# Turned keys, one-pass rounding and a new order in the merged attention of a six-sublayer decoder

## What is computed

```python
# causal self-attention in BitNet form, 16 query heads and 4 key heads of 32
def bitlinear(x, W):
    sw = mean(abs(W)) + 1e-05
    Wq = clip(round(W / sw), -1, 1) * sw
    sx = 127.0 / clip(max(abs(x), axis=-1), 1e-05, None)
    return (clip(round(x * sx), -128, 127) / sx) @ Wq.T
q, k, v = bitlinear(x, Wq), bitlinear(x, Wk), bitlinear(x, Wv)   # then rope on q and k
out = bitlinear(softmax(q @ k.T / sqrt(32), causal) @ v, Wo)

# gated attention to the memory of the same sequence (ctx), 16 heads of 32, mask on the memory
xr = rmsnorm(x, norm_w)
q, k, v = xr @ wq.T, ctx @ wk.T, ctx @ wv.T
out = sigmoid(xr @ wg.T) * (softmax(q @ k.T * 32 ** -0.5, mask) @ v @ wo.T)

# experts: 8 groups of 8, top 8 of 64 per token
soft = softmax(where(flat == 0, -1e9, flat))           # routing weights of a group
xg = x + soft @ mask_up_w                              # the "mover", 8 rows a group
y = sum over groups: scalar * ((silu(xg @ gate.T) * (xg @ up.T)) @ down.T)
```

## Time and profile before

| | |
|---|---|
| time, median of 3 runs (lowest to highest) | 3289.37 us (3287.53 to 3293.52) |
| profiled execution, its own time | 3293.45 us |
| its span, mean granted clock of PE | 3291.6 us, 0.939 |
| PE busy | 2859.2 us, 87% |
| PE's weight loads busy | 1596.8 us, 49% |
| DVE busy | 1998.1 us, 61% |
| ACT busy | 1622.2 us, 49% |
| POOL busy | 1209.3 us, 37% |
| 512-column matmul in an expert group, mean of 768 | 379 ns |
| `stage_moe`: first work of DVE | 2343.75 us |
| `stage_moe`: POOL's low part of the first weights ends, scores are ready | 2387.0 us, 2394.8 us |

### The profile page before, as it was taken

One profiled execution on the slowest core, in us unless ns is written; L12 is line 12 of the kernel. 1 busy time (PEld: TensorE's weight loads), 2 busy tenths in 40 slices (PEclk: granted clock), 3 DMA queues, 4 the chain that ended last, 5 costly groups with the idle time before them and its releaser, 6 DMA issues. The chain is left out here.

```text
span 3291.6 us, 48914 instructions
## 1 busy us (share of the span) xinstructions
PE 2859.2 (87%) x16626; PEld 1596.8 (49%) x16626; DVE 1998.1 (61%) x3760; ACT 1622.2 (49%) x3728; POOL 1209.3 (37%) x1236
## 2 busy tenths in 40 slices
PE   6789877999999997899368888877569999999998
PEld 4676744555555553344245444543434444444443
DVE  5778978877887876774678778764532212222224
ACT  7999955555555553642467666654321221212111
POOL 4888967554554541342321111100402221222211
PEclk8999988999999999999579999998779999999999
DMA  4111122000000001200300000000000000000001
GB/s 150 54 42 40 49 77 79 7 4 7 7 4 7 7 0 56 98 1 1 108 12 8 8 7 7 8 11 1 31 30 30 30 30 1 30 30 30 1 1 51
DMA packets 29926, 94.83 MB, mean 29 GB/s; under 512 B 3862, under 2 KB 4246, under 8 KB 26519
## 3 DMA queue, kind: packets, MB, share of 16 engines
q1 hardware_dynamic: 29718, 92.26, 8.2%
HBM read 87.79 MB, written 4.46 MB: 28 GB/s over the span
## 5 line engine op out<-in xcount | busy, mean ns | idle before, releaser
L710 POOL TENSOR_TENSOR m_aTl<-m_prod,m_aTh 128x512 bf16<-128x512 f32 x96 | 110.9, 1156 | 704.6 <-ACT m_aTh L764 704.6
L923 DVE TENSOR_TENSOR m_prod<-m_bank,m_gated 128x512 f32<-128x512 f32 x96 | 66.4, 692 | 497.1 <-ACT m_gated L762 497.1
L1893 POOL TENSOR_TENSOR s_state<-s_state,s_ct 128x512 f32<-128x512 f32 x256 | 326.6, 1301 | 85.0 <-DVE s_state L2068 83.1
L2068 DVE TENSOR_TENSOR_SCAN s_state<-s_decay,s_psd 128x512 f32<-128x512 f32 x256 | 301.9, 1209 | 68.3 <-PE s_psd L2213 35.0
L762 ACT ACTIVATE m_gated<-m_bank 128x512 f32<-128x512 f32 x96 | 57.2, 596 | 575.6 <-PE m_bank L1007 575.6
L1005 PE MATMUL m_bank<-m_xTh,m_wh 128*128 128x512 bf16 x768 | 291.1, 379 | 0.0
L1006 PE MATMUL m_bank<-m_xTl,m_wh 128*128 128x512 bf16 x768 | 291.1, 379 | 0.0
L1007 PE MATMUL m_bank<-m_xTh,m_wl 128*128 128x512 bf16 x768 | 291.1, 379 | 0.0
L2213 PE MATMUL s_psd<-ident,s_v 128*128 128x128 f32 x1024 | 165.3, 286 | 42.8 <-DVE s_state L2068 22.4
L1969 ACT ACTIVATE s_decay<-s_dt,s_nega 128x508 f32<-128x508 f32 x256 | 182.0, 712 | 20.5 <-DVE s_state L2068 20.3
L1982 ACT ACTIVATE s_v<-s_uT,s_bT 128x512 f32<-128x512 f32 x256 | 182.5, 714 | 0.8 <-PE s_psd L2213 0.7
(11 more groups left out here) (502 smaller groups left out, 8058.9 us busy)
## 6 DMA issues: line engine op xcount, KB each, us to landing
m_stage<-in_moe_w_dram SPq DMA_DIRECT2D x8, 2352.0 KB, 8.5
s_ct<-ssm_bc SPq DMA_DIRECT2D x64, 256.0 KB, 3.1
X<-in_x_dram SPq DMA_DIRECT2D x4, 1024.0 KB, 11.2
a_cf<-in_ctxT_dram SPq DMA_DIRECT2D x16, 256.0 KB, 2.6
a_wstage<-in_xa_wq_dram SPq DMA_DIRECT2D x8, 512.0 KB, 3.5
a_wstage<-in_xa_wo_dram SPq DMA_DIRECT2D x8, 512.0 KB, 3.8
f_wstage<-in_ffn_wg_dram SPq DMA_DIRECT2D x4, 1024.0 KB, 7.4
f_wstage<-in_ffn_wu_dram SPq DMA_DIRECT2D x4, 1024.0 KB, 5.7
```

The source lines that it names most:

```text
L1893: pool.tensor_tensor(h, h, ct[t % 4][:, s * P:(s + 1) * P].unsqueeze(1).broadcast_to([P, KB, P]), ALU.mult).then_inc(weighted, 1)
L2068: dve.tensor_tensor_scan(state[i % RING][:, :], decay[t % 2][:, s, :, :].rearrange("p m t -> p (m t)"), ps_d[i % 2][:, :], 0.0, ALU.mult, ...
```

## The change

Three things in `stage_pair`. First, the memory half's keys and queries come out of PE already turned (`turned_product`: 48 matmuls of 128 columns, the weight matrix as the stationary operand); `krow`, `qrow`, `turn_keys` and `turn_queries` are gone. High and low part are one pass of 128 x 512 each, into a dense buffer `kT`, and SP moves four row blocks of it into the block-diagonal buffer by DMA (`place_keys`). The causal half's rotated key is written to `krd`, four blocks of 128 columns with head h at columns 32h of block h and zeros elsewhere; PE turns the four blocks (`turn_key`), and high and low part are one pass of all 128 rows each. Second, `PairQuantizer`: ACT scales and rounds in one pass (`round`), DVE does both clips in one (`clip`), ACT takes `ROUND` off as before. Third, the hand-written orders: `memory_end` goes from quarter 2 to quarter 3, `values` and `key_low` of the causal half, `keys_low`, `queries_low`, `memory_values`, `gate_output`, `norm_apply`, `quantize_x` and the vector parts of both norms change their quarter or their place in it.

In `stage_moe`, `group_rows` is cut into `soft_rows`, done two thirds of a quarter earlier, and `mover_rows`; the mover of group 0 is made during the routing; the last `down_tile`s are spread over blocks 1 and 2 of the last quarter; and the last four tiles are normalised and stored one by one (`tail`) in place of one quarter.

```diff
+        def tiles_behind(q, b, last):
+
+            if last and q == TQ - 1:
+                return ((), (0, 1), (2, 3))[b]
+            return ((0, 1), (2, 3), ())[b]
...
-            for q in range(TQ):
+            for q in range(TQ - 1):
                 sp.wait_ge(ln.normed.sem, ln.normed.at(q))
                 sp.dma_start(out[4 * q:4 * q + 4].rearrange("s p d -> p s d"), fr.X[:, 4 * q:4 * q + 4, :]).then_inc(stored, 16)
-            sp.wait_ge(stored, 16 * TQ)
+            for t in range(4):
+                sp.wait_ge(tail.steps.sem, tail.steps.at(t))
+                sp.dma_start(out[SEQS - 4 + t], fr.X[:, SEQS - 4 + t, :]).then_inc(stored, 16)
+            sp.wait_ge(stored, 16 * (TQ + 3))
...
+                        if q == 2 and b == 0 and not last:
+                            soft_rows(g + 1, 1 - j)
                     if q == 0 and not last:
                         w_high_part(g + 1, 1 - j)
                     if q == 2 and not last:
-                        group_rows(g + 1, 1 - j)
+                        mover_rows(g + 1, 1 - j)
...
+            dve.wait_ge(padded, 4)
...
+            mover_rows(0, 0)
...
+                    if q == 1 and not last:
+                        soft_rows(g + 1, 1 - j)
                     if q == 2 and not last:
-                        group_rows(g + 1, 1 - j)
+                        mover_rows(g + 1, 1 - j)
...
-            ln.vector_end(dve, TQ - 2)
             for t in range(4):
                 add_tile(G - 1, TQ - 1, t, 1)
-            dve.wait_ge(added.sem, added.at(G - 1))
-            ln.vector(dve, TQ - 1)
-            ln.vector_end(dve, TQ - 1)
+                if t == 0:
+                    ln.vector_end(dve, TQ - 2)
+                dve.wait_ge(added.sem, added.at(G - 1, 4 * (TQ - 1) + t + 1))
+                tail.statistics(dve, t)
+                if t:
+                    tail.vector_end(dve, t - 1)
+            tail.vector_end(dve, 3)
...
-        self.kdh = [sb(f"{tag}_kdh{j}", [P, key_groups, 4, P], BF16, st) for j in range(2)]
-        self.kdl = [sb(f"{tag}_kdl{j}", [P, key_groups, 4, P], BF16, st) for j in range(2)]
+        self.kd = [sb(f"{tag}_kd{j}", [P, 2, 4, key_groups, P], BF16, st) for j in range(2)]
...
+                   (self.kd[p][:, 0, :, k, :], self.kd[p][:, 1, :, k, :]), False, True)
...
+            def place_keys(n, j):
+                sp.wait_ge(mk_low.sem, mk_low.at(n))
+                if late(n, 2):
+                    sp.wait_ge(mcore.scored.sem, mcore.scored.at(n - 2))
+                for h in range(4):
+                    rows = slice(32 * h, 32 * h + 32)
+                    sp.dma_start(mcore.kd[j][rows, :, h, :, :], kT[rows, :, :, :]).then_inc(mcore.k_ready.sem, 16)
...
+                    place_keys(2 * i + j, j)
+                    context(2 * i + j + 2)
...
-                for g in range(4):
-                    rows = slice(32 * g, 32 * g + 32)
-                    a = act.activation(core.kdh[j][rows, 0, g, :], bank[2][rows, 0:P], ACT.Copy)
-                a.then_inc(k_high.sem, 1)
+                act.activation(core.kd[j][:, 0, :, 0, :].rearrange("p h t -> p (h t)"), bank[2][:, :], ACT.Copy).then_inc(k_high.sem, 1)
...
-                act.activation(krow[:, :], bank[0][:, :], ACT.Copy).then_inc(k_row.sem, 1)
-
-            def queries(n):
-                act.wait_ge(mproj.sem, mproj.at(n, 3))
-                if late(n, 1):
-                    act.wait_ge(mq_turned.sem, mq_turned.at(n - 1))
-                act.activation(qrow[:, :], bank[2][:, :], ACT.Copy, scale=PairCore.HW ** -0.5).then_inc(q_row.sem, 1)
+                    act.wait_ge(mcore.k_ready.sem, mcore.k_ready.at(n - 1))
+                act.activation(kT[:, 0, :, :].rearrange("p c t -> p (c t)"), bank[0][:, :], ACT.Copy).then_inc(mk_high.sem, 1)
+
+            def queries_high(n, j):
+                act.wait_ge(mproj.sem, mproj.at(n, 2))
+                act.activation(mcore.qTh[j][:, :, :].rearrange("p g t -> p (g t)"), bank[2][:, :], ACT.Copy,
+                               scale=PairCore.HW ** -0.5).then_inc(mq_high.sem, 1)
...
+                            qx.round(act, s + 2, fr.X[:, s + 2, :])
...
+                            queries_high(m + 1, o)
+                    if g == 2:
                         if live(s - 1):
-                            copy_output(s - 1)
+                            qo.scalar(act, s - 1)
                         if live(m + 1):
-                            gates(m + 1, o)
+                            memory_values(m + 1, o)
+                    if g == 3 and live(m + 2):
+                        squares(m + 2)
...
+                    if g == 1 and live(s + 2):
+                        qx.scalar(act, s + 2)
+                    if g == 2 and live(m + 2):
+                        context_high(m + 2, p)
+                    if g == 3 and live(m + 1):
+                        gates(m + 1, o)
...
-                for g in range(4):
-                    rows = slice(32 * g, 32 * g + 32)
-                    a = dve.tensor_tensor(core.kdl[j][rows, 0, g, :], bank[2][rows, 0:P], core.kdh[j][rows, 0, g, :], ALU.subtract)
-                a.then_inc(core.k_ready.sem, 1)
+                dve.tensor_tensor(core.kd[j][:, 1, :, 0, :].rearrange("p h t -> p (h t)"), bank[2][:, :],
+                                  core.kd[j][:, 0, :, 0, :].rearrange("p h t -> p (h t)"), ALU.subtract).then_inc(core.k_ready.sem, 1)
...
+                dve.tensor_tensor(kT[:, 1, :, :].rearrange("p c t -> p (c t)"), bank[0][:, :],
+                                  kT[:, 0, :, :].rearrange("p c t -> p (c t)"), ALU.subtract).then_inc(mk_low.sem, 1)
...
-                    if g == 1 and live(s - 1):
-                        output(s - 1)
+                    if g == 1:
+                        if live(m + 1):
+                            keys_low(m + 1)
+                        if live(s - 1):
+                            output(s - 1)
+                        if live(s + 2):
+                            qx.clip(dve, s + 2)
                     if g == 2:
+                        if live(s - 1):
+                            qo.clip(dve, s - 1)
                         if live(s - 2):
-                            ln.vector_end(dve, s - 2)
+                            ln.statistics(dve, s - 2)
                         if live(s + 1):
                             query_low(s + 1, o)
-                    if g == 3 and live(s + 3):
-                        quantize_x(s + 3, o)
+                            key_low(s + 1, o)
+                    if g == 3 and live(s - 2):
+                        ln.vector_end(dve, s - 2)
                     if live(s):
                         core.low_part(dve, s, g)
                     if g == 0:
                         if live(s + 1):
                             rotate_keys(s + 1, o)
+                            values(s + 1, o)
                         if live(s - 1):
                             core.divide(dve, s - 1, o)
-                        if live(s + 1):
-                            values(s + 1, o)
-                    if g == 1 and live(s - 2):
-                        ln.statistics(dve, s - 2)
-                    if g == 2 and live(s + 1):
-                        key_low(s + 1, o)
+                    if g == 3 and live(s + 3):
+                        quantize_x(s + 3, o)
 
                     if live(m) and (g < 3 or live(m + 1)) or g == 3 and live(m + 1):
                         mcore.maxima(dve, *following(m, g, p)[:2])
                     if g == 0 and live(m - 1):
                         mcore.divide(dve, m - 1, o)
-                    if g == 1 and live(m - 1):
-                        low(oTl[:, :], bank[1][:, :], oTh[:, :], o_high, m - 1, o_low)
-                    if g == 2 and live(m - 1):
-                        gate_output(m - 1, o)
+                    if g == 1:
+                        if live(m - 1):
+                            low(oTl[:, :], bank[1][:, :], oTh[:, :], o_high, m - 1, o_low)
+                        if live(m - 2):
+                            mln.vector_end(dve, m - 2)
                     if g == 3:
-                        if live(m - 1):
-                            mln.vector_end(dve, m - 1)
                         if live(m + 2):
                             norm_mean(m + 2)
+                        if live(m - 1):
+                            gate_output(m - 1, o)
                     if live(m):
                         mcore.low_part(dve, m, g)
                     if g == 0 and live(m + 1):
                         low(nTl[o][:, :], bank[1][:, :], nTh[o][:, :], n_high, m + 1, n_low)
+                    if g == 1 and live(m + 1):
+                        queries_low(m + 1, o)
+                    if g == 2 and live(m + 1):
                         memory_values(m + 1, o)
-                    if g == 1 and live(m + 1):
-                        keys_low(m + 1, o)
-                    if g == 2:
-                        if live(m + 1):
```

(51 more changed lines are left out.)

301 lines of the change are left out of this document (157 added, 144 removed).

## The result

The changed kernel takes 3197.76 us (median of four runs, 3190.47 to 3201.64), the kernel before 3291.30 beside it. The ratio is 0.9714, 95% interval 0.9694 to 0.9735: 93.5 us less. The forecast was 3204, range 3158 to 3238.

A forecast was written before the change was run, and what follows sets the result against it. No engine full: full attention turns bound by queue order and cross-engine waits, late turns by latency, expert groups by PE's waits. Attention -59 and experts -27 make -86 us, from 3293.5 to 3208, as median 3204; range 3158 to 3238.

The forecast's parts named there:

- The keys: Key and query pieces in stage_pair: ACT -3.4 us, DVE -2.6 us a turn; turned matmuls 0.056 us each, DMAs cost nothing.
- Quantisation: Two quantisers in stage_pair: DVE loses a 0.53 us pass in each, -1.0 us; ACT gains two of 0.60.
- The ring: Waits across DVE and PE in a full stage_pair turn: 13.2, 11.1 and 13.4 us, sum 37.7 against 40.7.
- The stretches around it: Other stage_pair turns: two behind the full ones -5 us, two before -4, four early -4, three late -20.7.
- Groups: Seven expert groups in stage_moe: PE's waits of 1.58 and 0.75 us go, -16.3 us in all.
- Start of the experts: Before the first expert group: soft rows' turning earlier, -6.9 us; net with DVE's added wait -5.3 (-3 to -8).
- four memsets: Before the first expert group: DVE waits for all of POOL's memsets, +1.6 us.
- End: Last tiles of stage_moe: last `X` at 3283.1 for 3287.0, last store 2.6 us for 4.3; -5.6 us (-4 to -7).
- B: stage_pair order better than the schedule: DVE keeps only present waits, 34.5 us a turn, total 3156 us; chance 0.22.
- C: PE's 2.4 us idling in quarter 1 slows the Q product: +2 us on thirteen turns, total 3230; chance 0.13.
- D: Turned products in stage_pair limited by weight loads of 0.098 us each: +2.0 us a product, total 3242; chance 0.08.
- E: Key DMAs land late and hold the scores of quarter 3: slower than before, total 3316 us; chance 0.03.

The follow-up runs named there:

- keys_pieces: Changed kernel with the memory half's turned key placed by four 32-row pieces on ACT and on DVE, without kT and DMAs: 3252.61 us, ratio 0.9896.
- wide: Changed kernel with the memory half's K and Q as twelve 512-column matmuls each, keys and queries not turned: 3193.10 us, ratio 0.9702.
- quant_old: Changed kernel with the old quantisation, two clip passes on DVE and no rounding on ACT: 3203.62 us, ratio 0.9744.
- after_again: The changed kernel itself, unaltered, run again for a second trace: 3196.09 us, ratio 0.9705.
- pair_only: Changed kernel with stage_moe as in the kernel before: 3227.24 us, ratio 0.9832.
- end_stats: Changed kernel with memory_end before the memory half's low part (quarter 3) and ln.statistics behind its maxima (quarter 2): 3156.48 us, ratio 0.9607.
- mover_late: Changed kernel with the first group's mover made behind its soft rows again: 3206.58 us, ratio 0.9754.
- stats_late: Changed kernel with ln.statistics moved in quarter 2 behind the memory half's maxima: 3190.02 us, ratio 0.9710.

## Why the prediction was right, point by point

- **The keys.** The removed pieces were most of the gain of the attention; `keys_pieces` shows it for the memory half. Price and place were right: 0.68 for each dense pass, DMAs hidden with 10 us to spare (2.0 us to land, 2.6 was taken), 0.056 us for a turned matmul. The Trainium skill's figure of about 81 ns for a sustained stream (TensorE: Matmul & The Clock Gate, "Back-to-back issue gap") does not hold for these 48, and `wide` confirms that nothing is lost on them. Less was taken from DVE than the sum has: over the nine full turns its busy time fell by 3.1 us each, where 3.6 was added up, and ACT's by 2.1 (2.2).
- **Quantisation.** `quant_old` gives 0.9 us a turn at the upper clock, for 1.06 us more of DVE; it was taken at 1.0. That ACT's two passes are free, as assumed, fits this, but it was not tested by itself.
- **The ring.** Forecast 37.7 us a full turn, measured 37.4, and its three pieces are within 0.6 us of the schedule. The experiments that load or relieve its parts move a turn at the upper clock by what was added or taken: +1.06 (measured +0.9), +2.7 (+2.9 over all nine), -2.1 (-2.1), -1.0 (-1.1). The two idle times of DVE and the wait of PE at `bank[2]` stand where they were put.
- **The stretches around it were sized less well, and cancelled.** Full turns -29.4 (forecast -27). Turns before them -13.4 (-8). The two behind -3.0 (-5). Late turns -14.9 (-20.7), of which 3.3 is the clock in turn 17: `after_again` has -18.3. The stage: -59.6 (-59) in this trace and -64.3 in `after_again`. That the stage came out within 1 us is luck in part.
- **Groups.** -16.4 for seven waits of 2.33, as forecast. The other 2 us are a single step of 107.99 us in the trace of before that does not recur in the one after.
- **Start of the experts.** -8.9, forecast -5.3 (-3 to -8). The soft rows' product starts 6.9 us earlier, as added up. The 1.6 us for four memsets were a wrong term: DVE's first work did come 1.66 us later, but the scores are ready after 53.9 us, as in `pair_only` without that wait (53.8), and in the kernel before after 55.5. Their distance is 52.9 to 57.9 us in five of the traces, the longest in `keys_pieces` at a granted clock of 0.63, and `pair_only` has the 1.6 us without any edit of `stage_moe`: they can't be put down to the mover. Left out of the sum, though named as the far end of its range, were 3.3 us from the upper clock level at the routing; and left out altogether were 2.9 us the other way, since the first group then starts at the lower level. -6.9, -1.6, -3.3 and +2.9 make -8.9. The undoing of this one step cost 7.5.
- **End.** -6.5, forecast -5.6: the last `X` 4.3 us earlier (3.9), and 2.4 us from there to the end in place of 4.6 (1.7 less was forecast, 2.2 it is).
- **The rivals.** B (34.5 a turn) did not happen, but was reachable: `end_stats` is at 34.2. C is real: in four turns of `mover_late` PE fell to the lower level at the end of 2.22 us of idling or soon after 2.37, at 1.5 to 1.7 us each, near the price given (+2). It strikes some turns of some executions and not all thirteen: none of the nine full turns in the first trace of the changed kernel, one in `after_again`, four in `mover_late`. D is out. E comes with 32 DMAs and is far off with four.

## What to carry to other kernels

In these traces an elementwise pass costs its columns, not its rows (0.69 us for 32x512, 0.68 for 128x512 on DVE): four passes over 32 rows for a block layout are worth replacing by one dense pass and a few DMAs, as long as the number of DMAs times 0.63 us of issue fits into the time until the data is wanted.

When no engine is full, draw the ring of waits through all engines once and add it up; then look for idle time on the engine that forms most of it, and move work there that stands after the idle time and isn't wanted soon. Work in front of such a gap lengthens the turn even though the engine "has time". Count on the clock to blur the result: `stats_late` shortened the ring and gained nothing.

An engine without idle time in one stretch is not the bound for that reason; take something out of the stretch and see whether the idle time only comes back in another place.

## What the runs showed of the hardware that was not expected

- The length of PE's last idle time does not alone say whether its clock falls. After 2.22 us in the third full turn it stayed at the upper level in the changed kernel (0.63 us for the four transposes at 1823.47) and fell in `mover_late` (0.93 at 1826.59), with the same instructions ahead in the turn (but a stretch at the lower level in the turn before). After 2.37 us it stayed in the changed kernel (1861.56). In late turn 17 the first matmuls after 2.14 us of idling still take 0.38 us, and the fall comes about 1.3 us later, in the middle of a run of matmuls:

```profile
2196.43 0.39 PE L3216 MATMUL c_pss<-c_mcur,c_one 128*128 128x512 bf16 x1 [2.14 <-ACT c_prob L2460]
...
2197.52 0.38 PE L1736 MATMUL b_bank<-c_wvl,c_cTh 128*128 128x512 bf16 x1
2197.73 0.58 PE L1737 MATMUL b_bank<-c_wvh,c_cTl 128*128 128x512 bf16 x1
```

- 24 small matmuls during a wait left the next transposes of PE at the upper level: 1.94 us for sixteen against 3.62 without them, and 5.47 against 7.09 for the 32 products behind (`mover_late`). The price came later: in both traces of the changed kernel the first group's matmuls start at 0.58 or 0.63 us, and at 0.38 in `mover_late`.
